# First chunk of the delta rule of layer 2: without the products and the fills of its zero state

## The reference

```
    def _L1_attn_ref(x, ...):
        ...
        def step(S, ins):
            q_t, k_t, v_t, a_t, b_t, g_t = ins
            kkT = k_t[:, :, None] * k_t[:, None, :]
            trans = a_t[:, :, None] * (I - b_t[:, :, None] * kkT)
            vkT = v_t[:, :, None] * k_t[:, None, :]
            S = jnp.einsum('bij,bjk->bik', S, trans) + b_t[:, :, None] * vkT
            o = jnp.einsum('bc,bcd->bd', q_t, S) * g_t
            return (S, o)
        ...
        S0 = jnp.zeros((Bn, Cn, Cn), x.dtype)
        _, o = jax.lax.scan(step, S0, (...))
        y = jnp.swapaxes(o, 0, 1) @ Wo + bo
        return y
...
    x = x + _L1_attn_ref(xn, ...) + _L1_ffn_ref(xn, ...)
```

## Time and profile before

| | us |
|---|---|
| median of 3 runs | 640.13 |
| lowest and highest of the runs | 639.52, 640.41 |
| the profiled execution's own time | 638.06 |
| its span, from the first to the last instruction | 636.2 |

### The profile page before, as it was taken

One profiled execution on the slowest core, in us unless ns is written; L12 is line 12 of the kernel. 1 busy time (PEld: TensorE's weight loads), 2 busy tenths in 40 slices (PEclk: granted clock), 3 DMA queues, 4 the chain that ended last, 5 costly groups with the idle time before them and its releaser, 6 DMA issues. The chain is left out here.

```text
span 636.2 us, 10166 instructions
## 1 busy us (share of the span) xinstructions
PE 542.6 (85%) x3552; PEld 426.4 (67%) x3552; DVE 456.5 (72%) x797; ACT 393.3 (62%) x771; POOL 378.3 (59%) x296
## 2 busy tenths in 40 slices
PE   5999966587787878888798988898899998989997
PEld 2444565476575767566675856798688986776776
DVE  6799799999999998897273887443333576648662
ACT  4679799869979987455369774513211234747670
POOL 0578779989999996487550930474910671224530
PEclk9999679799899899999899998999999999999999
DMA  5035054345676650200070010430611210000002
GB/s 130 4 75 116 12 120 105 83 109 130 135 138 132 134 119 2 76 0 2 13 201 14 2 11 8 99 106 32 187 32 40 69 34 2 2 1 0 2 1 67
DMA packets 45820, 40.46 MB, mean 64 GB/s; under 512 B 12183, under 2 KB 32585, under 8 KB 45770
## 3 DMA queue, kind: packets, MB, share of 16 engines
q1 hardware_dynamic: 44746, 37.71, 25.1%
q0 software_dynamic: 1024, 2.10, 1.1%
HBM read 33.70 MB, written 6.09 MB: 63 GB/s over the span
## 5 line engine op out<-in xcount | busy, mean ns | idle before, releaser
L435 PE MATMUL bank<-all_ident,l0s_ring 128*128 128x128 f32 x512 | 71.9, 288 | 19.2 <-POOL l0s_ring L731 19.1
L435 PEld LDWEIGHTS bank<-all_ident,l0s_ring 128*128 128x128 f32 x512 | 60.8, 148 | 28.2 <-POOL l0s_ring L731 25.7
L860 DVE TENSOR_TENSOR_SCAN l0s_ring<-l_XM,l0s_ring,bank 128x512 f32<-128x512 f32 x62 | 74.7, 1255 | 1.8 <-PE bank L415 1.8
L731 POOL TENSOR_TENSOR l0s_ring<-l0s_ring,all_XF 128x1024 f32<-128x1024 f32 x31 | 66.3, 2158 | 8.7 <-issue 4.8
L415 PE MATMUL bank<-all_ident,all_XNT 128*128 128x128 f32 x312 | 50.5, 303 | 23.2 <-DVE l0s_ring L860 18.4
L731 POOL TENSOR_TENSOR l0s_ring<-l0s_ring,l0s_c_rest 128x1024 f32<-128x1024 f32 x32 | 65.4, 2066 | 6.2 <-DVE l0s_ring L860 3.5
L607 ACT ACTIVATE all_XNT<-l_wraw,l_wins 128x256 f32<-128x256 f32 x156 | 66.2, 498 | 0.5 <-PE bank L415 0.4
L860 DVE TENSOR_TENSOR_SCAN l0s_ring<-bank,l0s_ring 128x512 f32<-128x512 f32 x50 | 60.2, 1244 | 4.0 <-POOL l0s_ring L721 2.4
L415 PEld LDWEIGHTS bank<-all_ident,all_XNT 128*128 128x128 f32 x312 | 38.9, 155 | 30.6 <-issue 15.7
L586 ACT ACTIVATE l_XM<-l_DT,l_negA 128x512 f32<-128x512 f32 x78 | 50.8, 712 | 0.6 <-DVE l0s_ring L860 0.6
L721 POOL TENSOR_TENSOR l0s_ring<-l_DTU,l0s_b_all 128x1024 f32<-128x1024 f32 x20 | 40.2, 2009 | 0.0
(11 more groups left out here) (441 smaller groups left out, 1511.2 us busy)
## 6 DMA issues: line engine op xcount, KB each, us to landing
l0s_c_rest<-bc_rows SPq DMA_DIRECT2D x16, 512.0 KB, 5.4
all_XF<-bc_rows SPq DMA_DIRECT2D x16, 512.0 KB, 5.3
l0s_b_all<-bc_rows SPq DMA_DIRECT2D x20, 256.0 KB, 6.1
l_wall<-in_L_ffn_W SPq DMA_DIRECT2D x14, 256.0 KB, 4.7
all_X<-in_L_attn_x SPq DMA_DIRECT2D x4, 256.0 KB, 3.4
gx<-l1m_TD SPq DMA_DIRECT2D x1, 1024.0 KB, 5.2
gy<-l1m_TD SPq DMA_DIRECT2D x1, 1024.0 KB, 8.6
out<-all_X SPq DMA_DIRECT2D x4, 256.0 KB, 3.1
```

Source lines behind the costliest of these rows:

```text
L435: last = nc.tensor.matmul(y_of(k, j), hc[n % CRING][:, j, bass.ts(k, P)], S.ident[:, :], start=False, stop=(n % DS == DS - 1 and k % 2 == ...
L731: nc.gpsimd.tensor_tensor(hc[n % CRING][:, :, :], h(n)[:, :, :], wide(c_wide[p % HRING][:, n % 2, :]), ALU.mult).then_inc(hc_ready, 1)
L860: nc.vector.tensor_tensor_scan(h(n)[:, j, :], factor, added, before, ALU.mult, ALU.add).then_inc(h_ready, 1)
```

## The change

Chunk 0 no longer uses a state. The two `memset` are gone, with the semaphore `zeroed` and the waits for it. In `carry(0)` PE makes only the two products from KVA and TT; in `products(0)` it leaves out SS times QG, and `outputs(0)` starts bank 5 itself. On DVE, `states(0)` copies the two banks into ST1 and SS1 in place of scaling and adding. All other chunks are as they were.

```
-                        nc.gpsimd.memset(ST[0][:, :], 0.0)
-                        nc.gpsimd.memset(SS[0][:, :], 0.0).then_inc(zeroed, 1)
...
+                            if c == 0:
+                                nc.tensor.matmul(S.bank[0][:, 0:P], TT[:, c, :], KVA[:, c, P:2 * P], start=True, stop=True).then_inc(u_done, 1)
+                                nc.tensor.matmul(S.bank[1][:, 0:P], KVA[:, c, P:2 * P], TT[:, c, :], start=True, stop=True).then_inc(ut_done, 1)
+                                return
                             nc.tensor.matmul(S.bank[0][:, 0:P], TT[:, c, :], KVA[:, c, P:2 * P], start=True, stop=False)
                             nc.tensor.matmul(S.bank[1][:, 0:P], KVA[:, c, P:2 * P], TT[:, c, :], start=True, stop=False)
-                            if c:
-                                pe.wait_ge(st_new, c)
+                            pe.wait_ge(st_new, c)
...
                             if c:
                                 pe.wait_ge(og_ready, c)
                                 pe.wait_ge(ss_new, c)
-                            pe.wait_ge(qg_ready, c // TPB + 1)
-                            nc.tensor.matmul(S.bank[5][:, 0:P], SS[r][:, :], QG[:, bass.ts(c, P)], start=True, stop=False)
+                                pe.wait_ge(qg_ready, c // TPB + 1)
+                                nc.tensor.matmul(S.bank[5][:, 0:P], SS[r][:, :], QG[:, bass.ts(c, P)], start=True, stop=False)
...
-                            nc.tensor.matmul(S.bank[5][:, 0:P], KVA[:, c, 0:P], PT[r][:, :], start=False, stop=True).then_inc(o_done, 1)
+                            nc.tensor.matmul(S.bank[5][:, 0:P], KVA[:, c, 0:P], PT[r][:, :], start=(c == 0), stop=True).then_inc(o_done, 1)
...
-                        pe.wait_ge(zeroed, 1)
                         for c in range(BEFORE):
...
                             dve.wait_ge(s_done, 2 * c + 1)
-                            if c:
-                                dve.wait_ge(st_new, c)
-                                dve.wait_ge(ss_new, c)
+                            if c == 0:
+                                nc.vector.tensor_copy(ST[1 - r][:, :], S.bank[2][:, 0:P]).then_inc(st_new, 1)
+                                dve.wait_ge(s_done, 2 * c + 2)
+                                nc.vector.tensor_copy(SS[1 - r][:, :], S.bank[3][:, 0:P]).then_inc(ss_new, 1)
+                                return
+                            dve.wait_ge(st_new, c)
+                            dve.wait_ge(ss_new, c)
...
-                        dve.wait_ge(zeroed, 1)
```

More of the change, by code:

```diff
@@ L1907, in layer1_phases @@
                 xhi, xlo = ([ph.sb(f"{n}{i}", [P, BLK], F32R) for i in range(2)] for n in ("xhi", "xlo"))
-                (loaded, zeroed, u_done, ut_done, u_ready, ut_ready, s_done, st_new, ss_new, p_done, p_ready, o_done, og_ready, yo_done) = (
-                    ph.sem(n) for n in ("loaded", "zeroed", "u_done", "ut_done", "u_ready", "ut_ready", "s_done", "st_new", "ss_new", "p_done",
+                (loaded, u_done, ut_done, u_ready, ut_ready, s_done, st_new, ss_new, p_done, p_ready, o_done, og_ready, yo_done) = (
+                    ph.sem(n) for n in ("loaded", "u_done", "ut_done", "u_ready", "ut_ready", "s_done", "st_new", "ss_new", "p_done",
                                         "p_ready", "o_done", "og_ready", "yo_done"))
```

## The result

| | kernel before | changed kernel |
|---|---|---|
| median of 5 runs each, us | 639.88 | 644.19 |
| lowest and highest | 638.41, 640.41 | 642.74, 644.33 |
| the profiled execution's own time | 638.06 | 644.29 |
| its span | 636.2 | 642.2 |

The ratio is 1.006, with an interval of 1.0037 to 1.0084: slower by 0.4 to 0.8%. The prediction was 641.1 us with a range to 642.1. The result lies outside it.

A forecast was written before the change was run, and what follows sets the result against it. It took the path at the change to be the rows' DMA, then PE's turning, DVE's copy and the first expert's products. Direct 0 plus clock fall +1.0 us, added to the 640.13 us median, gave 641.1 us; range 639.0 to 642.1.

The forecast's parts named there:

- direct terms: At the two early chunks: work removed ahead of PE's wait for the rows, worth 0 us (-0.2 to +0.1).
- earlier start: PE's first product of the phase, no longer waiting for the fill of SS0, comes 0.44 us earlier (0 to 0.48).
- PE through the chunks: PE finishes the two early chunks 1.04 us earlier, bounds 0.6 and 1.3.
- none of it is on the path: The rows' DMA still lands at 451.75 us and sets PE's next product, so 0 of the 1.04 us counts.
- idle stretch of 2.95 us: PE's wait for the rows after chunk 1 grows from 1.91 us to about 2.95 us.
- mechanism: PE's longer idle stretch before the rows makes its clock fall in most executions; cost 0.5 to 1.28 us, chance 0.38.
- price of a fall: Low clock over the 16 transposes of rows after the wait: +1.0 us, from +0.5 to +1.6.
- margin for the scatter: Allowance for differences between runs: 0.4 us to either side of the median of the kernel before.
- slower beyond the bound: Rival: clock falls just as the rows land, slowing turning and first expert's products; +1.6 us, 641.7 us, chance 0.20.
- cheap case: Fall begins while PE still waits for the rows, so over 1 us of low clock costs nothing; +0.5 us left.
- Hidden and nothing else: Rival: the clock stays up at the wait for the rows, so no change; 640.1 us, chance 0.32.
- Faster: Rival: rows land before the chunks are done, so 1.04 us comes through; 639.0 us, chance 0.10.

The follow-up runs named there:

- late rows: Kernel before with six small loads of wqkv and bias issued ahead of the rows' DMA: 646.55 us against 639.54, ratio 1.0109.
- the first comparison: Changed kernel against the kernel before, five runs each, no further edit: 644.19 us against 639.88, ratio 1.006.
- the second comparison: Changed kernel run again without edit, against the kernel before: median 641.77 us (637.59 to 644.98), ratio 1.0017.
- the filled kernel before: Kernel before with 12 transposes that nobody reads put into PE's wait for the rows: 639.27 us, ratio 0.9993 to the kernel before.
- the kernel with the fills back: Changed kernel with the two memset on POOL and the zeroed waits on PE and DVE put back: 640.35 us, ratio 1.0002 to the kernel before.

## Why the prediction was wrong, and what of it was right

**The direct terms were right.** The earlier start was put at 0.44 us and is the 0.44 us by which PE's wait shrank (1.89 to 1.45); PE through the chunks 1.04 us earlier: 1.02. That none of it is on the path: the DMA ends PE's wait in all three traces of the changed kernel. The idle stretch of 2.95 us: 2.85, 3.11 and 2.76.

**The mechanism held at the place, with an open end.** The clock falls at that wait in three of three traces of the changed kernel and in none of three of the kernel before, and late rows bring it on in that one too. Where the rows' DMA was cut and the wait was 0.58 us, it didn't fall there, in either trace, with the change in place. That the length of the wait alone decides isn't shown, and other waits speak against it. In the second trace the fall began 1.5 us into the wait. In the first trace of the changed kernel a wait of 3.14 us that ends at 104.66 is followed by full clock, and in the kernel before a wait of 1.86 us is followed by a fall.

**The step that failed is a size, in two terms: the price of a fall, and the margin for the scatter.** First the price. I took +1.0 us from the transposes after 313.31, with a top of 1.6 us, because I let the low stretch be 3.2 us long and counted only the turning. That row was a milder case than I read in it: by the trace's clock the fall there came at 314.04, so that the first 0.7 us of the transposes ran at full speed, and of the 3.4 us of low clock (to 317.45) the last part lay on products that I didn't count. At the place it cost 1.5 us twice and 4.0 us once, 2.3 us on average (20.18 - 17.87, the means of the table's three traces each). In two traces it came as the rows landed, so that the turning alone lost 1.6 us; this is the rival "slower beyond the bound", priced at +1.6 us and given 0.20. In the third it began inside the wait, as the forecast's cheap case had it, and held for 10 us. The trace of before had rows that should have warned me: 0.50 over the whole 4.5 us of 124.3 to 128.8, with 0.79 in the wait ahead, and 0.50 from 86.4 to 90.0. Those are parts of two low stretches of 6.8 us (122.89 to 129.72, and 85.35 to 92.17), at two of those three waits of over 3 us. Half of 6.8 us is 3.4 us; with that as the top and the 0.4 us of scatter the range would have reached 643.9 us.

**The scatter was taken from three runs.** 0.4 us to either side became the range's margin. In 35 runs the kernel before goes from 636.5 to 643.6 us. In the first comparison this term did the greater harm: in the execution that was traced the fall cost 1.5 us where I had put 1.0, a miss of 0.5 us, and 4.5 us of the difference came from elsewhere. The 641.77 us of the second comparison lie inside my range, a hit that owes as much to chance as the first miss. The scatter is also why 4.3 us were measured at first where the traces give the place 1.5 to 4.0 us. In the first trace of the changed kernel 4.5 us lie elsewhere; the second trace has 1.6 of them too, at 567 us, but nothing ahead of the phase. The fall near 567 us isn't tied to the change either: the filled kernel before has one at 563.7 us. What the three comparisons say of the changed kernel together is 1.006, 1.0017 and 1.0024, each above 1. Two of these intervals hold 1, so that the loss is 2 us rather than 4 us is my reading of them with the traces, not a measured number. Why all five of the first runs came out high stays open.

**The other rivals.** "Hidden and nothing else" (0.32) described the one trace of the kernel with the fills back, not the changed one. "Faster" needed rows that land before 450.3; when the DMA was cut, 1.05 us came through at the place, though the times of the two cut kernels don't resolve it.

## What to carry to other kernels

Work removed ahead of a wait that something else ends isn't free: it turns into idle time, and where PE's idle stretch grew from some 2 us to some 3 us here, the clock fell in three traces of three, and the work behind the wait paid. So ask of each such saving what ends the wait, and move that too: with the rows' DMA cut in four the same change brought its 1 us at the place, and this is the one version here that was clearly faster in a comparison (0.9924, for cut and change together; in the other it was 0.9984 and not resolved). And where the clock falls differently in each execution, compare lengths of a stretch in several traces before believing a difference of a few microseconds in the median.

## What the runs showed of the hardware

- The clock fell 1.5 us into a wait of 3.11 us and stayed low for 10 us (0.50 in all three windows from 450.6 to 460.7), though PE had been at work again since 452.15; at the end of waits of 2.85 and 2.76 us it fell for 3.4 us, about the time of the turning.
- The length of a wait alone didn't tell whether the clock falls. Waits of 3.14 us (changed kernel, ended at 104.66) and 3.01 us (kernel before, second trace, ended at 104.08) had no fall; waits of 1.86 to 2.00 us in the first trace of the kernel before were followed by one four times, 0.7 to 1.3 us after PE had started again. And in that trace the clock was low from 68.28 to 78.52 with no wait of PE over 0.7 us from 60 us on.
- Where in the program the clock falls differs between executions of one and the same kernel. In the three traces of the changed kernel layer 0 ends at 315.4, 312.1 and 311.3 us; the falls in it differ in place and number from trace to trace.
- A kernel's time differed by 25 us, or 4%, between chips. In the slower one's trace of the kernel before PE ran its products a few at a time from 429 to 442 us, with pauses ended by nothing that the profile shows:

```profile
431.81 0.50 PE L1555 MATMUL bank<-l1at_TT,l_wall 128*128 128x128 f32 x3 [1.13 <-issue]
...
433.94 1.07 PE L1553 MATMUL bank<-l_wall,l1at_TT 128*128 128x128 f32 x3 [1.13 <-issue]
436.05 1.49 PE L1553 MATMUL bank<-l_wall,l1at_TT 128*128 128x128 f32 x3 [1.03 <-issue]
```

  What made PE pause there is open.
